# Differential attention with a split-precision pipeline: the slot's order of transposes, products and combination changed

## The reference

```
Q1,Q2 = split(X Wq^T)   K1,K2 = split(X Wk^T)   V = X Wv^T      (per head, d_head 128, V 256 wide)
A1 = softmax(Q1 K1^T / sqrt(128))   A2 = softmax(Q2 K2^T / sqrt(128))
attn = A1 - lam * A2                                   lam: one number per head
O = attn V ;  O = O / sqrt(mean(O^2) + eps) * rms_scale * (1 - lambda_init)
x = layernorm(x + concat_heads(O) Wo^T)
```

## Time and profile before

| what | value |
|---|---|
| time, median of three runs | 1060.2 us (1058.76 to 1063.17) |
| the profiled execution's own time | 1051.25 us |
| its span | 1049.5 us |
| TensorE busy | 888.1 us (85%) |
| GpSimd busy | 795.6 us (76%) |
| VectorE busy | 764.1 us (73%) |
| ScalarE busy | 581.7 us (55%) |
| TensorE's granted clock, mean | 0.926 of full speed |

### The profile page before, as it was taken

One profiled execution on the slowest core, in us unless ns is written; L12 is line 12 of the kernel. 1 busy time (PEld: TensorE's weight loads), 2 busy tenths in 40 slices (PEclk: granted clock), 3 DMA queues, 4 the chain that ended last, 5 costly groups with the idle time before them and its releaser, 6 DMA issues.

```text
span 1049.5 us, 15335 instructions
## 1 busy us (share of the span) xinstructions
PE 888.1 (85%) x4365; PEld 718.0 (68%) x4366; DVE 764.1 (73%) x1183; ACT 581.7 (55%) x1090; POOL 795.6 (76%) x874
## 2 busy tenths in 40 slices
PE   6789999999999999999999999999999732386700
PEld 5577778787877788778877887878788631165500
DVE  6777788877887878788778877888788547574303
ACT  3556667666766576656765666766676331143100
POOL 2567878887888798888888888888799753377762
PEclk9999999999999999999999999999999955599755
DMA  2000000000000000000000000000000152012223
GB/s 71 1 11 11 1 1 22 1 1 0 20 0 0 10 10 0 0 10 10 0 0 10 10 0 0 10 0 0 1 1 1 47 137 65 19 51 36 27 26 87
DMA packets 31856, 18.57 MB, mean 18 GB/s; under 512 B 4512, under 2 KB 30272, under 8 KB 31824
## 3 DMA queue, kind: packets, MB, share of 16 engines
q1 hardware_dynamic: 26192, 13.85, 4.8%
q0 software_dynamic: 5632, 4.33, 3.0%
HBM read 12.80 MB, written 5.37 MB: 17 GB/s over the span
## 4 chain that ended last, share of the span: by engine, by line
PE 53%; issue 17%; DVE 16%; POOL 7%; DMA 4%; ACT 3%; POOLq 0%; DVEq 0%; ACTq 0%; SPq 0%
PE t_ps L1061 7%; DVE negmax L750 6%; PE ring_a L994 5%; PE ring_b L994 5%; PE ring_a L996 5%; PE ring_a L995 5%; PE ring_b L996 4%; PE ring_b L995 4%; PE u_ps L994 4%; PE u_ps L996 4%; PE u_ps L995 4%; POOL acc_dram L491 3%; DMA acc_dram<-at,idx 2%; POOL prob L482 2%; ACT prob L562 2%
## 5 line engine op out<-in xcount | busy, mean ns | idle before, releaser
L449 POOL TENSOR_TENSOR at_lo<-at,at_hi 128x1024 fp32r<-128x1024 f32 x127 | 308.5, 2429 | 0.8
L562 ACT ACTIVATE prob<-ring_a,negmax 128x1024 f32<-128x1024 f32 x128 | 142.9, 1116 | 253.4 <-DVE negmax L750 253.4
L421 POOL TENSOR_TENSOR s1sq<-psum 128x1 f32<-128x1 f32 x127 | 104.4, 822 | 122.0 <-ACT at L570 120.4
L818 DVE SCALAR_TENSOR_TENSOR attn<-prob,coef 128x1024 f32<-128x1024 f32 x128 | 181.7, 1419 | 5.0
L750 DVE TENSOR_REDUCE negmax<-ring_b 128x1 f32<-128x1024 f32 x128 | 155.6, 1216 | 4.1 <-PE ring_b L996 1.2
L750 DVE TENSOR_REDUCE negmax<-ring_a 128x1 f32<-128x1024 f32 x128 | 155.6, 1216 | 1.1
L562 ACT ACTIVATE prob<-ring_b,negmax 128x1024 f32<-128x1024 f32 x128 | 143.0, 1117 | 19.5 <-DVE negmax L750 17.7
L424 POOL TENSOR_SCALAR at_hi<-at 128x1024 fp32r<-128x1024 f32 x127 | 142.4, 1122 | 0.0
L1061 PE MATMUL t_ps<-ident,attn 128*128 128x128 f32 x1024 | 133.7, 273 | 3.2 <-DVE attn L818 2.8
L1061 PEld LDWEIGHTS t_ps<-ident,attn 128*128 128x128 f32 x1024 | 118.3, 141 | 25.9 <-DVE attn L818 11.9
L570 ACT ACTIVATE at<-t_ps 128x1024 f32<-128x1024 f32 x128 | 130.3, 1018 | 2.0 <-PE t_ps L1061 2.0
(11 more groups left out here) (239 smaller groups left out, 1703.2 us busy)
## 6 DMA issues: line engine op xcount, KB each, us to landing
at<-in_L_ffn_w SPq DMA_DIRECT2D x16, 256.0 KB, 3.3
xres<-in_L_attn_X SPq DMA_DIRECT2D x2, 512.0 KB, 4.4
wq_s<-in_L_attn_Wq SPq DMA_DIRECT2D x8, 128.0 KB, 2.1
wk_s<-in_L_attn_Wk SPq DMA_DIRECT2D x8, 128.0 KB, 2.3
wv_s<-in_L_attn_Wv SPq DMA_DIRECT2D x8, 128.0 KB, 2.1
wo_s<-in_L_attn_Wo SPq DMA_DIRECT2D x8, 128.0 KB, 2.3
xg_dram<-xres SPq DMA_DIRECT2D x2, 512.0 KB, 3.4
acc_dram<-xres SPq DMA_DIRECT2D x2, 512.0 KB, 5.2
```

The lines of the kernel that those rows point to most:

```text
L421: pool.tensor_tensor(s1sq[:, r % TPH:r % TPH + 1], s1, s1, ALU.mult).then_inc(s1sq_ready, 1)
L449: pool.tensor_tensor(at_lo[:, g, :, c], src, at_hi[:, g, :, c].bitcast(F32), ALU.subtract).then_inc(at_split, 1)
L562: act.activation(prob[:, par, m, :], ring[m][:, :], ACT.Exp, bias=negmax[:, par, m:m + 1], accum_out=sums).then_inc(prob_ready, 1)
L818: dve.scalar_tensor_tensor(out=attn[:, par, :], in0=prob[:, par, 1, :], scalar=coef[:, par:par + 1], in1=prob[:, par, 0, :], op0=ALU.mult, ...
```

## The change

The second bank of `t_ps` becomes `x_ps`, a bank for query and weight products alone, and only the first bank takes transposes. A tile is transposed in two halves of four through this one bank, and each half is copied by itself. On TensorE the halves stand between the score groups. The products stand at the end of the slot, one chunk of 512 columns at a time (`X_QB`, `X_M`, `X_WT`, `X_WP`, `X_QA`), and are split in the following slot. On VectorE the combination `attn` is made one slot later (`LAG_S = 1`) and stands behind the second maximum; the transposes follow a further slot later (`LAG_T = 2`). ScalarE copies both halves ahead of the exponentials, and squares at the head of the slot. GpSimd makes `var_o` and `fac` first, and `es1` once for four tiles.

```diff
-    LAG_T = 1
+    LAG_S = 1
+    LAG_T = 2
-    AT_QB, AT_WT, AT_WP, AT_M, AT_QA = (1, 2), 4, 6, 9, (11, 13)
+    X_QB = {0: (0, 0), 2: (0, 1), 3: (1, 0), 4: (1, 1)}
+    X_M, X_WT, X_WP, AT_WW = 6, 7, 8, 10
+    X_QA = {10: (0, 0), 11: (0, 1), 12: (1, 0), 14: (1, 1)}
+        x_ps = t_ps[:, NC:2 * NC]
...
         @block.gpsimd, slot(): var_o and fac of tile i - LAG_Y first, then
+                r = i - LAG_T
+                    pool.wait_ge(t_copied, 2 * (tt + 1))
+                    pool.tensor_tensor(s1sq[:, r % TPH:r % TPH + 1], s1, s1, ALU.mult).then_inc(s1sq_ready, 1)
+                        pool.tensor_scalar(at_hi[:, g, :, c], src, 1.0, 0.0, ALU.mult, ALU.add).then_inc(at_hi_done, 1)
+                        pool.wait_ge(at_hi_done, tt + 1)
+                        pool.tensor_tensor(at_lo[:, g, :, c], src, at_hi[:, g, :, c].bitcast(F32),
+                                           ALU.subtract).then_inc(at_split, 1)
+                    if r % GT == GT - 1:
+                        pool.tensor_tensor(es1[:, g4], s1sq[:, g4], eps_c[:, 0:1].broadcast_to([P, GT]),
+                                           ALU.mult).then_inc(es1_ready, 1)
...
         @block.scalar, slot(): u_hi, the square, ww_hi and ww_lo, then
+                def at_copy(half):
+                    r = i - LAG_T
+                    if exists(h, r, first) and r < TPH:
+                        tt = t - LAG_T
+                        act.wait_ge(t_ready, 2 * tt + half + 1)
+                        need(act, at_split, tt - 1)
+                        act.activation(at32[:, r % 2, half * NC:(half + 1) * NC], t_ps[:, 0:NC],
+                                       ACT.Copy).then_inc(t_copied, 1)
+                at_copy(0)
+                if not tail and i - 1 in X_QB:
+                    q_round(h, "b", *X_QB[i - 1], x_ps)
+                if not last and i - 1 in X_QA:
+                    q_round(h + 1, "a", *X_QA[i - 1], x_ps)
+                at_copy(1)
                 (the two exponentials)
...
         @block.vector, slot(): u_lo, row_max(0), xres, splits of what stands in x_ps, then
+                    row_max(1)
+                r = i - LAG_S
+                if exists(h, r, first) and r < TPH:
+                    ts, sp = t - LAG_S, r % 2
+                    dve.wait_ge(prob_ready, 2 * ts + 2)
+                    (rs2, coef as before, of tile ts)
+                    need(dve, t_ready, 2 * (ts - 1))
+                    dve.scalar_tensor_tensor(out=attn[:, sp, :], in0=prob[:, sp, 1, :],
...
         @block.tensor, slot():
+                def transposes(half):
+                        if half == 0:
+                            pe.wait_ge(attn_ready, tt + 1)
+                        need(pe, t_copied, 2 * tt + half)
+                        for k in range(GT):
+                            kk = half * GT + k
+                            last_t = pe.transpose(t_ps[:, k * P:(k + 1) * P], attn[:, r % 2, kk * P:(kk + 1) * P],
+                                                  ident[:, :])
+                        last_t.then_inc(t_ready, 1)
+                    scores(0, 0)
+                transposes(0)
+                    scores(0, 1)
+                    scores(1, 0)
+                transposes(1)
+                    scores(1, 1)
                 (the six u matmuls, then the product that is due in slot i into x_ps, then o)
```

More of the change, by code:

```diff
@@ L410, in slot @@
                 t = TPH * h + i
[L411 to L425, removed]
-                if exists(h, r, first) and r < TPH:
[L429 to L437, removed]
+                r = i - LAG_Y
+                if exists(h, r, first) and r < TPH:
+                    tt, par = t - LAG_Y, r % 2
+                    pool.wait_ge(es1_ready, GPH * h + r // GT + 1)
                     pool.wait_ge(ssq_ready, tt + 1)
-                    pool.tensor_tensor(var_o[:, par:par + 1], ssq[:, par:par + 1], es1[:, par:par + 1],
+                    pool.tensor_tensor(var_o[:, par:par + 1], ssq[:, par:par + 1], es1[:, r % TPH:r % TPH + 1],
                                        ALU.add).then_inc(var_ready, 1)
@@ L820, in slot @@
                                              op0=ALU.mult, op1=ALU.add).then_inc(attn_ready, 1)
-                q_lower(1)
+                if i == 0 and not first:
+                    head_lambda()
                 if tail and i == TPH - 1 + LAG_T:
@@ L1025, in slot @@
                     q = slice(qt * P, (qt + 1) * P)
[L1026 removed]
+                    if c == 0:
                         need(pe, prob_ready, 2 * (t - 1) + m + 1)
[L1030 to L1035 removed]
@@ L1037, in slot @@
                         if i == 0:
[L1038 removed]
+                            pe.wait_ge(q_split, q_count(h, "a", m, NCH - 1))
                         if i == QT:
[L1040 to L1049 removed]
@@ L1051, in slot @@
+                if not tail:
+                    scores(0, 0)
                 if first and i == 0:
@@ L1083, in slot @@
                         need(pe, u_split, g)
-                    times_x(0, PER // 2)
-                put_in = [i == AT_QB[0] and not tail, i == AT_QA[0] and not last, i == AT_WP and not tail,
-                          i == AT_M and not last]
-                if any(put_in):
-                    pe.wait_ge(prob_ready, 2 * t + 1)
-                if put_in[0]:
-                    q_product(h, "b", (0,))
-                if put_in[1]:
-                    q_product(h + 1, "a", (0,))
-                if put_in[2]:
-                    for m in range(2):
-                        last_w = pe.matmul(ring[0][:, 0:D], wv_s[:, m, :], wot_s[:, m, :],
+                    for k in range(j * PER, (j + 1) * PER):
+                        last_u = three(u_ps[:, :], xk_hi[:, b * KT + k, :], xk_lo[:, b * KT + k, :],
+                                       at_hi[:, gb, k, :], at_lo[:, gb, k, :],
+                                       start=(k == 0), stop=(k == KT - 1))
@@ L1098, in slot @@
+                if i == X_WP and not tail:
+                    pe.wait_ge(wt_split, 3 * (h + 1))
+                    for m in range(2):
+                        last_w = pe.matmul(x_ps[:, 0:D], wv_s[:, m, :], wot_s[:, m, :],
                                            start=(m == 0), stop=(m == 1))
                     last_w.then_inc(wp_ready, 1)
-                if put_in[3]:
-                    m_product(h + 1)
-                r = i - LAG_U
-                if exists(h, r, first) and r < TPH:
-                    last_u = times_x(PER // 2, PER)
-                    if r % GT == GT - 1:
-                        last_u.then_inc(u_ready, 1)
+                if i in X_QA and not last:
+                    m, c = X_QA[i]
+                    if m or c:
+                        pe.wait_ge(q_split, q_count(h + 1, "a", m, c) - 1)
+                    else:
+                        pe.wait_ge(wp_split, h + 1)
+                        pe.wait_ge(m_split, h + 2)
+                    q_product("a", m, c, x_ps)
```

258 lines of the change are left out of this document (111 added, 147 removed).

## The result

The changed kernel takes 1320.95 us (median of four, 1318.86 to 1322.96) against 1059.72 for the kernel before, run beside it: 1.2456 times as long, interval 1.2424 to 1.2489. The forecast was 1307.

What follows compares the result with a forecast made beforehand. TensorE, with 98.9 us of work in one head's 100 us, was taken as the bound. Profiled execution 1051.25 + 217 for longer slots + 30 for the clock + 9 to the median = 1307 us; range 1150 to 1370.

Steps and rivals of the forecast that it cites:

- loop: In every slot attn stands behind the second row maximum and the next slot's transposes wait for it: 6.14 us at least.
- collision: GpSimd's at_lo, issued 0.41 us ahead of VectorE's attn, holds the shared SBUF port: slots of 7.94 us, chance 0.74.
- T: Start of a slot's first four transposes on TensorE; the next slot's was put at T+7.94.
- 3.1 us or more: Sign of a right forecast: attn's mean length, in place of 1.40, each ending 1.09 us after an at_lo.
- the state repeats itself: GpSimd, with 5.3 us of work per 7.94 us slot, isn't late for the next round, so at_lo goes first again.
- Sum of the slots: First transposes at 29.9, then 126 x 7.94 = 1000; last tile's transposes at 1034 against 817.10: +217 us.
- The clock: TensorE's idle gaps bring half clock in eight slots a head, six in ten, 0.85 us each: 30 us, bounds 0 and 107.
- (1): Rival: attn wins the port from at_lo, slots of 6.14 us, 1079 us in all; chance 0.09.
- (2): Rival, a mix: half of the slots collide, 7.04 us a slot, 1165 us in all; chance 0.12.
- (3): Rival: TensorE stays the bound and the 33 us of waits are gained, 1027 us in all; chance 0.04.
- (4): Rival: the clock falls in every slot, 1384 us in all; chance 0.03.
- The part that was left at nothing: TensorE's 33 us of waits around the products, for a score bank or split: removed, but worth nothing as TensorE waits elsewhere.

Runs made afterwards that it cites:

- Experiment 4: Changed kernel with six useless matmuls of 512 columns ahead of each slot's first transposes, none in the tail: 1282.23 us, 1.2127 times the kernel before.
- experiment 5: Changed kernel with at_lo cut to the first of its eight blocks, output not the reference's: 1073.72 us, 1.0141 times the kernel before.
- experiment 1: Changed kernel with one wait more: GpSimd issues at_lo only when the slot's attn is done: 1152.68 us, 1.0874 times the kernel before.
- experiment 3: Changed kernel with attn back in the slot of its own tile's exponentials (LAG_S = 0), all else kept: 1060.61 us, 1.0012 times the kernel before.
- 7: The version of experiment 3 with xres moved behind the second maximum on VectorE: 1062.36 us, 1.004 times the kernel before.
- experiment 8: The version of 7 with ScalarE's square also moved behind its first copy: 1060.11 us, 1.003 times the kernel before.
- 9: Changed kernel with the transposes and all behind them one slot later (LAG_T = 3), attn left in place: 1038.26 us, 0.9869 times the kernel before.
- 10: The version of 9 with at_lo issued as two half-size instructions: 1028.82 us, 0.9762 times the kernel before.
- experiment 2: Changed kernel with at_lo issued as two half-size instructions, order kept: 1151.32 us, 1.0888 times the kernel before.

## Why the prediction was right

Four kernels show the cause as a product: with loop and collision 1321 us (1282 with the clock held up); the loop without the collision 1074; the collision without the loop 1038; the kernel before, which has no such loop and, in 41 tiles, short collisions, 1060. Neither is dear alone.

**The steps inside the slot.** Each was read off one ordinary slot; here they stand beside those of the slot at 412.81. Second transposes: T+1.81 forecast, T+1.87 measured. `at_lo` issued: T+4.40, T+4.48. `attn` issued: T+4.81, T+4.93. Margin: 0.41, 0.45. `at_lo` over: T+6.80, T+6.87. `attn` behind it: 1.09, 1.08. Next T: T+7.94, T+8.00. The first four transposes took 0.41 us to the next matmul where 0.35 was taken, which shifts both sides. The hop to the second maximum was 0.12 us where 0.03 was taken, which delays `attn` alone. Over the 96 slots without half clock the margin is 0.29 to 1.12 us, with a median of 0.53, and never changes its sign. `attn` comes that much later where VectorE has more to do ahead of it, and is held the shorter for it: its mean is 2.85 us, short of the "3.1 us or more" that I had named as a sign. The end of `at_lo`, and with it the slot, does not move. That the state repeats itself held to the end: in 126 of the 128 tiles `attn` was issued while an `at_lo` ran, in all but the first and the last.

**Sum of the slots.** First T, first T of the tail, and the last tile's transposes, in TensorE's timeline of the changed kernel:

```profile
30.10 1.12 PE L1044 MATMUL t_ps<-ident,attn 128*128 128x128 f32 x4 [1.23 <-DVE attn L815]
...
1075.27 0.66 PE L1044 MATMUL t_ps<-ident,attn 128*128 128x128 f32 x4 [2.41 <-DVE attn L815]
...
1080.28 0.91 PE L1044 MATMUL t_ps<-ident,attn 128*128 128x128 f32 x4
```

The first was forecast at 29.9. From 30.10 to 1075.27 are 126 slots. I took their lengths from the ends of the 128 combinations: 96 have a mean of 8.005 us, and 30 are 8.8 to 9.7 us, 36 us above that together. So 126 x 8.005 = 1009 where 1000 was forecast, and 36 for the clock where 30 was. The tail to the last transposes took 5.0 in place of 3.75, and what follows them 4.4 us more than before (236.8 against 232.4, from each span). Together 9 + 6 + 1.3 + 4.4, some 21 us over the forecast of the profiled execution (1318.86 against 1298.25). The median lies only 2 us above that execution, where 9 were allowed. That leaves the 14 us by which 1307 was short.

**The clock.** That this sum was nearly right is luck: two errors cancelled. I had eight slots a head at six in ten, 38 in all, each losing 0.85 us. In heads 1 to 6 the long slots were only those behind a slot in which TensorE has no product (there are five a head); 19 of those 30 were long; the other 11 long slots belong to the first and the last head. All 30 lost 1.2 us on average. Where TensorE had stood idle for 1.71 us (472.02, behind the weight product) the clock stayed up. In the window at 462.50, behind 2.21 us, it was at its lower level from the first score matmul on, not "a little after", and still for the first matmul behind the second transposes, hence 1.2 and not 0.85. Experiment 4 puts the whole at 39 us. That an idle array falls to 1.2 GHz and activity brings it back is what the Trainium skill has ("TensorE: Matmul & The Clock Gate", on the clock gate); by the runs, activity that keeps it up may be work of no use.

**The rivals.** (1) 1079 was the price of the loop alone, and experiment 5 gave 1074 with the port free. That such a state would not hold by itself was not tried: experiment 1 forced it by a wait, and the wait's own ring put 79 us on the 1074. (2) There was no mix. (3) TensorE as the bound came only when the loop was taken out. (4) The clock fell in 30 slots, not in all.

**Cause of the price.** That `attn` is "nearly always first" in the kernel before was read too kindly: it is in 87 of 128 tiles, and in the others, but for one, it comes near the end of `at_lo`. The forecast doesn't rest on it. The rule cited from the Trainium skill ("SBUF — State Buffer", section "Who interferes with whom"), that issue order decides who blocks, agrees in each run: `attn` is 1.28 us when first (experiment 1) and 2.8 when second. The prediction's own rows gave what it needed beyond that, the 1.09 us.

**The part that was left at nothing.** The waits around the products did vanish, and nothing came of it in the changed kernel. Nor did it where the combination stood in its own slot again (experiments 3, 7 and 8), where I had counted on it: there a ring through VectorE and ScalarE, from one second maximum to the next, takes 6.19 us in experiment 3 and 6.22 in experiment 8 in slots with a `q_lo`. I had not looked for that ring in the kernel before, and the list of waits doesn't name it, since all of its links are short. What came of them, 14 and 23 us, came with the combination one slot later and the transposes two more (experiments 9 and 10).

## What to carry to other kernels

Before an operation is moved within a pipelined slot, write down for every engine what is issued when, counted from one event, and look for a ring: a chain that leads from an event to the same event one slot later. If its length comes near the slot, every delay inside it is paid once a slot, and one slot of lag more takes it out (1321 to 1038 us here, for a change of constants). Where a VectorE operation with two operands in SBUF runs beside GpSimd, see which one is issued first, and cut the holder's instruction where the order can't be changed.

## What the runs showed of the hardware

- A VectorE operation that waits for the port gets it at the next boundary between two GpSimd instructions, even when the next one is ready. With `at_lo` in two halves the three take turns: 1.28 us for the first half, 1.08 for `attn`, 1.15 for the second half, of the 3.51 from the start of the one half to the end of the other (experiment 2).
- GpSimd's smallest operations are held as well. `var_o`, one column, takes 0.19 us alone (412.80) and 1.17 beside a combination that holds the port (419.64), for it ends 0.05 us after that one does.
- More work made the kernel faster: 756 useless matmuls of 512 columns took 39 us off it (experiment 4), with the granted clock of the attention's windows at 1.00 where it had been 0.96 to 0.97.
